# When the query and key stacks of images 2 and 3, and the mode weights, are begun in a four-stage convolution kernel

## The reference, cut to what matters

```python
q = _conv(query, Wq[idx], 'SAME').reshape(n, HEADS, HC, -1)     # 4 heads of 8 channels, 1024 queries
k = _conv(token, Wk[idx], 'VALID').reshape(n, HEADS, HC, -1)    # 900 keys
v = _conv(token, Wv[idx], 'VALID').reshape(n, HEADS, HC, -1)
w = jax.nn.softmax(jnp.einsum('nhcq,nhcd->nhqd', q, k), axis=-1)
a = jnp.einsum('nhcd,nhqd->nhcq', v, w).reshape(n, CA, hh, ww)
...
block = compl_mul2d(x_ht[:, :, :MODES1, :MODES2], weights1)     # stage 4: the mode weights
```

## Time and profile before

| | |
|---|---|
| median of 3 runs | 372.82 us (371.9 to 374.68) |
| span of the profiled execution | 369.9 us |
| time of the profiled execution beside its span | not given; the median is 2.9 us above the span |
| TensorE busy | 311.3 us (84%) |
| VectorE / ScalarE / GpSimd busy | 229.8 us (62%) / 173.0 us (47%) / 44.0 us (12%) |
| mean granted clock of TensorE | 0.950 |

### The profile page before, as it was taken

How to read it: one execution, slowest core, us unless ns; L and a number is a source line. 1 busy time by engine, 2 the same in 40 slices (tenths; PEclk the granted TensorE clock), 3 DMA queues, 4 the chain that set the end, 5 groups by cost and what they waited for, 6 DMA issues and landing times.

```text
span 369.9 us, 5771 instructions
## 1 busy us (share of the span) xinstructions
PE 311.3 (84%) x2163; PEld 109.3 (30%) x2186; DVE 229.8 (62%) x494; ACT 173.0 (47%) x334; POOL 44.0 (12%) x44
## 2 busy tenths in 40 slices
PE   5599665688997556999999999999999799885994
PEld 1133111232342112333232323323232222333931
DVE  5980053834846662668786886777877221579945
ACT  2100000012335546978888787878878786300000
POOL 5000600400000000001010100101010102405100
PEclk9989966999999986999999999999999999998798
DMA  2799996000066953970000000000000000000001
GB/s 87 155 202 226 205 182 171 0 3 0 10 194 139 140 108 109 248 313 2 2 2 2 2 1 1 2 1 4 0 3 0 1 3 0 2 0 1 4 2 57
DMA packets 6283, 23.89 MB, mean 65 GB/s; under 512 B 1048, under 2 KB 1816, under 8 KB 5712
## 3 DMA queue, kind: packets, MB, share of 16 engines
q1 hardware_dynamic: 6000, 23.43, 26.3%
q0 software_dynamic: 256, 0.11, 0.2%
HBM read 11.59 MB, written 2.37 MB: 38 GB/s over the span
## 4 chain that ended last, share of the span: by engine, by line
PE 44%; DVE 10%; issue 5%; ACT 4%; another core or an unknown queue 0%; DVEq 0%; ACTq 0%
PE ps L1160 12%; PE ps L1178 12%; PE ps L1137 11%; DVE arena_a L461 3%; ACT arena_b L677 3%; PE ps L1290 2%; PE ps L1183 2%; PE ps L1233 2%; DVE mx L889 1%; PE ps L1250 1%; ACT relus L685 1%; DVE arena_a L965 1%; DVE sums L884 1%; PE ps L1298 1%; PE ps L1006 1%
## 5 line engine op out<-in xcount | busy, mean ns | idle before, releaser
L677 ACT ACTIVATE arena_b<-ps 128x512 f32<-128x512 f32 x232 | 125.2, 608 | 33.5 <-PE ps L1160 16.8
L1137 PE MATMUL ps<-arena_a 128*128 128x450 bf16 x256 | 86.1, 364 | 16.0 <-issue 11.5
L1160 PE MATMUL ps<-arena_a 128*128 128x512 bf16 x207 | 78.1, 386 | 1.0 <-ACT arena_b L677 0.4
L889 DVE TENSOR_REDUCE mx<-ps 128x1 f32<-128x450 f32 x120 | 69.2, 617 | 6.5 <-PE ps L1137 4.8
L884 DVE CUSTOM_DVE_ANT_0 sums<-ps,relus 128x450 bf16<-128x450 f32 x68 | 41.2, 625 | 40.5 <-PE ps L1137 31.1
L1178 PE MATMUL ps<-arena_b,vt 128*32 128x512 f32 x448 | 59.7, 605 | 0.7 <-ACT arena_b L677 0.7
L1160 PEld LDWEIGHTS ps<-arena_a 128*128 128x128 bf16 x224 | 21.6, 98 | 76.9 <-ACT arena_b L677 50.4
L685 ACT ACTIVATE relus<-ps 128x450 f32<-128x450 f32 x68 | 37.4, 556 | 11.0 <-PE ps L1137 10.9
L1006 PE MATMUL ps<-zeros 128*128 128x512 bf16 x109 | 29.0, 407 | 8.4 <-DMA xa<-x 3.5
L1137 PEld LDWEIGHTS ps<-arena_a 128*128 128x128 bf16 x256 | 23.8, 99 | 40.1 <-issue 10.7
L639 ACT ACTIVATE arena_b<-ps 96x386 f32<-96x386 f32 x3 | 1.5, 490 | 63.3 <-PE ps L1055 63.2
(11 more groups left out here) (131 smaller groups left out, 250.0 us busy)
## 6 DMA issues: line engine op xcount, KB each, us to landing
arena_b<-arena_a SPq DMA_DIRECT2D x12, 578.0 KB, 10.4
arena_b<-wmodes SPq DMA_DIRECT2D x1, 4096.0 KB, 22.0
arena_a<-k_scratch SPq DMA_DIRECT2D x3, 516.8 KB
arena_b<-arena_a SPq DMA_DIRECT2D x4, 306.0 KB, 5.6
arena_a<-q_scratch SPq DMA_DIRECT2D x3, 384.0 KB
arena_b<-arena_a SPq DMA_DIRECT2D x4, 272.0 KB, 5.0
k_scratch<-arena_b SPq DMA_DIRECT2D x3, 344.5 KB, 3.3
cst<-consts SPq DMA_DIRECT2D x1, 1029.0 KB, 11.1
```

Of the source, the lines that this page charges most:

```text
L677: nc.scalar.activation(probs[:, n % PRING, :], ps[:, SCORE_RING[n % len(SCORE_RING)], :], ACT.Exp).then_inc(expd, 1)
L889: nc.vector.tensor_reduce(mx[:, a, e:e + 1], bank, AX.X, ALU.max).then_inc(max_read, 1)
L1137: mm(ps[:, block_bank(i), 0:KHALF], qst[:, e, g, qt * P:(qt + 1) * P], kst[:, g, at:at + KHALF], start=True, stop=True).then_inc(max_score ...
L1160: last = mm(ps[:, bank, :], kst[:, g, t * P:(t + 1) * P], qst[:, e, g, :], start=True, stop=True)
```

## The change

A wait is added ahead of the stacks of images 2 and 3, for the turned maxima of s = 0, which also moves the second write of q and `stack_q(3)` behind it; the wait ahead of the mode weights is raised to the turned maxima of s = 1.

```diff
             stack_k(2, HEADS, 2 * HEADS)
             stack_q(1, 0, HEADS, 2 * HEADS)
+            sp.wait_ge(m_in, 16)
             stack_k(3, 2 * HEADS, G)
             stack_q(2, 0, 2 * HEADS, G)
             for s in range(PARTS):
...
             sp.wait_ge(qd_written[1], PARTS * 16)
             stack_q(3, 1, 0, G)
-            sp.wait_ge(m_in, 16)
+            sp.wait_ge(m_in, 2 * 16)
             sp.dma_start(wm, wmodes).then_inc(wm_loaded, 16)
```

## The result

The changed kernel takes **369.56 us** (median of 14 runs, 367.35 to 372.32), the kernel before 372.29 us in the runs beside it (14 runs, 370.44 to 374.88). The ratio is 0.9929 with a 95% interval of 0.99 to 0.9959: 2.7 us faster. The forecast was 372.5, and 0.3 us of change.

The account below looks back on a forecast made before the run. TensorE, busy nearly without a break, was taken to bound the attention. Image 2's block 2.1 us earlier less 1.8 us of half clock gave 0.3 off 369.9, 369.6; plus 2.9 to the median, 372.5 us; range 366.5 to 377.7.

Parts of the forecast that it names:

- both stalls: TensorE's idle times before image 1's first block (4.3 us) and before score 0 (5.9 us), forecast to be exchanged for 2.1 + 8.0.
- Stall A: TensorE's 4.3 us wait before image 1's first block; 0 to 4.3 us could be gained, the middle, 2.2, was taken.
- The stacks' rate: Stacks of images 2 and 3 after the new wait: 127 GB/s, 17.1 us plus 1.1 us start, landed at 149.3.
- The estimate of 4.6 + 2.5 + 1.1 us: Key stacks, query stacks and start at 27 GiB/s per DMA engine; the sum would then be a full 10 us of gain.
- When they are wanted: Image 2's first block: score 0 at 133.1 plus 8.2 us at full clock, so wanted at 141.3.
- The half clock: TensorE's clock granted at half behind the 8 us pause before image 2: plus 1.8 us, bounds 0 and 3.
- The rest of SyncE's list: Write of q, stack_q(3), later turned maxima and mode weights, all behind the stacks: no time lost.
- Rival 2: Stacks come a good deal earlier: 370.6 at 143 GB/s, 364.7 at 198; chance 0.21 of below 369.1.
- Rival 3: Stacks come before they are wanted, at 239 GB/s; all 10 us kept, 362.7; chance 0.04.
- Rival 4: First turned maxima's 9.8 us are not the queue's doing; 7.4 us slower, 380.2; chance 0.04.
- Rival 1: Stacks come later still, stall before image 1 unsaved or 100 to 116 GB/s: 376.7 or 379.7; 0.16 beyond 376.5.

Follow-up runs that it names:

- e9: The changed kernel with the write of q's second half ahead of the new wait, the stacks of images 2 and 3 behind it: 370.56 us, ratio 0.9944.
- e10: The changed kernel with the stacks of images 2 and 3 ahead of the new wait, only the write of q's second half behind: 371.53 us, 0.9988.
- e3: The changed kernel with the new wait on image 1's key and query stacks instead of the first turned maxima: 368.38 us, ratio 0.9883.
- e7: The changed kernel with 22 matmuls on zeros ahead of TensorE's wait for the stacks of images 2 and 3: 368.18 us, ratio 0.9887.
- e1: The changed kernel with the wait ahead of the mode weights back at the first turned maxima: 371.84 us, ratio 0.9965.
- e4: The changed kernel with the stacks behind the new wait split, image 2's first, then image 3's, with semaphores of their own: 362.45 us, ratio 0.9722.
- e11: The changed kernel with image 2's and image 3's stacks split behind the wait and q's second-half write ahead of it: 362.85 us, ratio 0.9736.
- e2: The kernel before with only the wait ahead of the mode weights raised to the second turned maxima: 372.01 us, ratio 0.9968.
- e8: The changed kernel with the new wait on image 1's key stacks alone: 367.99 us, ratio 0.9895.

## Why the prediction was right or wrong

The time forecast, 372.5, is 2.9 above the measured one. That is inside the wide range (366.5 to 377.7) and the band of 1%, but outside the 370.2 to 375 given as the forecast's own. The change itself was forecast at 0.3 us and measured at 2.7, with an interval of 1.5 to 3.7 that leaves 0.3 out; the other 0.5 of the 2.9 is that the kernel before took 372.29 in its new runs, not 372.82. The number is near because any such change is small beside 370 us. The mechanism came as forecast: both stalls named, the first turned maxima at 2.2 us (2.1), no stall at score 0, and one new pause before image 2's first block at a falling clock. The pause is 5.9 us, not 8. What was off are sizes.

- **Stall A**, forecast 2.2 us gained and 0.3 by the clock. Measured from the first key stack's issue, image 1's first block came 3.9 us sooner, and from it to the issue of the turned maxima it was 3.0 us in place of 3.1, at a granted clock of 1.00: 0.1 by the clock. (The idle time itself shrank by only 3.4, as image 0's blocks ended 0.6 us sooner.) The middle of 0 to 4.3 was too careful, as the two groups under e9 and e10 show.
- **The stacks' rate**, the term that was mis-sized. I took 127 GB/s, "that of the long stretch with the same rows", and got 18.2 us; it was 16.3 us, which is 2.18 MB / (16.3 - 1.1) = 143 GB/s, the bound from images 0 and 1. What I took for a property of these rows goes with their place in the queue: in their first 3.1 us e3 has the same rows at 142 GB/s, e10 at 78; and the 127 is itself the mean of a stretch with a dip to 73 in it. The estimate of 4.6 + 2.5 + 1.1 us that stands beside the prediction's sum was not met either: 16.3 us. With 143 GB/s and the 4.0 us of stall A the sum gives the block at 131.5 - 4.0 + 2.2 + 16.3 = 146.0, against 146.8 measured in an execution that began 0.8 us later.
- **When they are wanted**, forecast 141.3, measured 141.1 by two errors against each other: score 0 came at 131.5, 1.6 sooner than 133.1, and from there to the block it was 9.7 us without the pause, not 8.2, because VectorE and ScalarE still have the blocks of image 1 to read while the first scores run: the weight loads between 132.1 and 135.4 wait 0.18 to 0.60 us each for one of the two. In the kernel before these scores came after a stall, when the readers had caught up (both idle from 137.5 to 141.5).
- **The half clock**, forecast 1.8 us, measured 1.3 (4.3 against 3.0), 1.5 by e7, and 2.3 in the executions of e1 and e9.
- **The rest of SyncE's list**, forecast nothing. Right for the changed kernel: second maxima 6.5 us to landing, score 29 not stalled. But the reason given, that less stands beside them than before, hid that the raised weights' wait is what keeps it so. With it lowered (e1) 1.4 us are lost.
- **Rival 2**, the stacks at 143 GB/s, forecast 370.6 and had the mechanism and nearly the number. Rival 3 (all of the gain kept) was not met by a higher rate, but e4 met its condition with half the bytes, and came out at 362.45, near the 362.7 that it named. Since kernels before differ by up to 0.9 us between sessions (372.29 to 373.14), part of the agreement is luck. Rival 4 fell with the 2.2 us. Rival 1, late stacks, fell with the rate.

## What to carry to other kernels

A small transfer that somebody waits for lands behind whatever large ones are in flight when it is issued (2.2 us alone, 4.6 to 10.4 among stacks); hold back the large ones whose users are far off, and then ask when these are wanted, since a wait that is only moved is exchanged for another (e3 and the changed kernel). Cut the large transfer where its first user's share ends, and let each user wait for its own part: that was worth 7 us, more than twice the wait itself, while the cut without the wait was worth nothing that the times could show (0.9936 to 1.0003). Where executions differ in their start, count from an event just ahead of the change to one just behind it; "rest" agreed to 0.1 us in nine of thirteen kernels, and where it did not it showed a stall (1.4 us in e1, 0.4 in e11), the end of the half clock (0.4 in e9), or differences of 0.5 to 0.7 us behind the last turn (e7, e9, e11).

## What the runs showed that was not expected

Rows of 22 KB queued behind image 1's stacks ran at 64 to 78 GB/s for 3.1 us (before, e2 and e10), and the same rows issued once the queue was empty of image 1's key stacks at 142 to 166 GB/s in their first 3 us (e3, e8 and the changed kernel); rows of 11 KB queued early didn't show it there. No run isolates the cause. Behind the same pause of 6 us TensorE's granted clock was back near full after 3.1 us in one execution (0.94 in the 1.2 us that follow) and still at 0.50 after 5.3 us in two others. The mode weights landed 22.0 us after their issue beside stack_q(3) and 13.5 us behind it in the changed kernel.
